# Rotation parts over 29 slots, keys stored once, row stores on ScalarE's queue, maxima ahead of keys, scans and 2-byte tables in the routing

## What is computed

```python
xn = layernorm(x)
Q = (xn @ W_q)              # 16 heads of 16
K = (xn @ W_k)              # 4 heads of 16, each for 4 query heads
V = (xn @ W_v)
scores = rope(Q) @ rope(K).T / sqrt(16)
attn = softmax(scores) @ V @ W_o
top 2 of 8 experts by xn @ W_r, weights = softmax of the two logits
ffn = sum of weight * ((clip(silu(xn @ W_g[e])) * (xn @ W_u[e])) @ W_d[e])
out = x + attn + ffn
```

## Time and profile before

| | us |
|---|---|
| median of 3 runs | 575.77 (574.92 to 575.99) |
| profiled execution | 576.07 |
| its span | 574.3 |
| TensorE busy | 526.5 (92%) |
| VectorE busy | 396.3 (69%) |
| ScalarE busy | 383.5 (67%) |
| GpSimd busy | 173.2 (30%) |
| share of the chain that ended last: TensorE, VectorE, DMA | 73%, 12%, 6% |

### The profile page before, as it was taken

How to read it: one execution, slowest core, us unless ns; L and a number is a source line. 1 busy time by engine, 2 the same in 40 slices (tenths; PEclk the granted TensorE clock), 3 DMA queues, 4 the chain that set the end, 5 groups by cost and what they waited for, 6 DMA issues and landing times.

```text
span 574.3 us, 9921 instructions
## 1 busy us (share of the span) xinstructions
PE 526.5 (92%) x3464; PEld 249.3 (43%) x3464; DVE 396.3 (69%) x920; ACT 383.5 (67%) x548; POOL 173.2 (30%) x208
## 2 busy tenths in 40 slices
PE   1996748897999998999999999999999999999997
PEld 1832324454555554444444444444444444444433
DVE  4578756961666666587788887888888788785123
ACT  3421412431333433799999999999999999998673
POOL 3015854541222210012416422551344342600000
PEclk9997987897999999999999999999999999999999
DMA  8950235566642120310511421422224113100101
GB/s 293 375 184 1 80 133 170 169 183 193 170 138 74 59 62 29 103 38 19 131 47 45 115 58 41 102 65 75 57 58 119 31 57 84 30 2 21 46 29 55
DMA packets 39566, 53.72 MB, mean 94 GB/s; under 512 B 7936, under 2 KB 25728, under 8 KB 39520
## 3 DMA queue, kind: packets, MB, share of 16 engines
q1 hardware_dynamic: 32624, 40.25, 23.9%
q0 software_dynamic: 3408, 9.31, 5.9%
q10 hardware_dynamic: 3488, 3.55, 1.8%
HBM read 36.18 MB, written 16.65 MB: 92 GB/s over the span
## 4 chain that ended last, share of the span: by engine, by line
PE 73%; DVE 12%; DMA 6%; issue 3%; ACT 2%; SPq 2%; POOL 2%; DVEq 0%; ACTq 0%; POOLq 0%
PE bank L1249 21%; PE bank L1239 9%; PE bank L1112 9%; PE bank L1167 8%; PE bank L1129 7%; PE bank L1235 6%; PE bank L1184 4%; PE bank L1285 3%; DMA k_st<-rope_low 3%; PE bank L1122 2%; DMA rows_out<-xn 2%; DVE xn_t L907 2%; DVE xn L983 2%; SPq L378 1%; PE bank L1072 1%
## 5 line engine op out<-in xcount | busy, mean ns | idle before, releaser
L702 ACT ACTIVATE big<-bank 128x1024 f32<-128x1024 f32 x256 | 252.9, 1024 | 18.6 <-PE bank L1239 18.3
L1249 PE MATMUL bank<-big,v_st 128*32 128x256 f32 (+1 forms) x1472 | 148.3, 474 | 2.8 <-DVE xn L983 2.8
L1239 PE MATMUL bank<-qs,kb 64*128 64x512 f32 x512 | 120.0, 408 | 0.7 <-ACT big L702 0.7
L904 DVE TENSOR_REDUCE mx<-bank 128x1 f32<-128x512 f32 x128 | 87.8, 686 | 27.9 <-PE bank L1129 20.1
L899 DVE TENSOR_REDUCE mx<-bank 128x1 f32<-128x512 f32 x128 | 87.9, 687 | 22.1 <-PE bank L1114 20.0
L1167 PE MATMUL bank<-big,xn 128*128 x156 | 82.6, 654 | 15.9 <-ACT xn L671 15.4
L907 DVE CUSTOM_DVE_ANT_0 xn_t<-bank,xn_t 128x512 f32<-128x512 f32 x128 | 87.5, 684 | 4.5 <-PE bank L1129 1.5
L657 ACT ACTIVATE xn_t<-bank 128x512 f32<-128x512 f32 x128 | 76.7, 599 | 20.4 <-PE bank L1114 12.2
L1239 PEld LDWEIGHTS bank<-qs,kb 64*128 64x128 f32 x512 | 57.7, 185 | 19.4 <-ACT big L702 12.3
L1112 PE MATMUL bank<-ka,qs 64*128 64x512 f32 x128 | 63.4, 495 | 0.4 <-DVE mx L904 0.4
L1114 PE MATMUL bank<-ka,qs 64*128 64x512 f32 x128 | 63.3, 495 | 0.0
(11 more groups left out here) (140 smaller groups left out, 611.7 us busy)
## 6 DMA issues: line engine op xcount, KB each, us to landing
qs<-q_hl SPq DMA_DIRECT2D x64, 128.0 KB, 2.7
rows_out<-xn SPq DMA_DIRECT2D x39, 128.0 KB, 2.6
ka<-k_st SPq DMA_DIRECT2D x16, 256.0 KB
kb<-k_st SPq DMA_DIRECT2D x16, 256.0 KB
xs<-in_L_attn_x SPq DMA_DIRECT2D x4, 512.0 KB, 6.3
big<-in_L_ffn_Wg SPq DMA_DIRECT2D x16, 128.0 KB, 6.5
big<-in_L_ffn_Wu SPq DMA_DIRECT2D x16, 128.0 KB, 6.6
big<-in_L_ffn_Wd SPq DMA_DIRECT2D x16, 128.0 KB, 6.5
```

Of the source, the lines that this page charges most:

```text
L702: act.activation(probs[kt % 2][:, 2 * j:2 * j + 2, :].rearrange("p r q -> p (r q)"), st_ps[j][:, :], ACT.Exp, scale=1.0 / math.sqrt(HD)).t ...
L904: nc.vector.reduce_max(mx[h][:, STEPS + k, 1:2], max_bank(v, i), axis=X_AXIS).then_inc(mx_taken, 1)
L1239: last = mm(out[i], kb[p][half[i], kt // QT, keys], qs[q][half[i], j, :], start=False, stop=True, skip_group_check=kt % 2 == 1)
L1249: last = mm(o_ps[32 * r:32 * (r + 1), columns], v_st[p][:, key_block(kt), :], probs[kt % 2][:, r, columns], start=(kt == 0 and columns.sta ...
```

## The change

- A part of the rotation is done in each of slots 1, 3, 5, 7, 9, 11, 14, 17, 20, 23, 26, 29, in four buffers (NB = 4). The order of parts goes by batch. Block 3 is projected partly in slots 0 and 1 and copied by ACT in slot 2.
- A key part is now 128 rows of 512 columns: its lower 64 rows are the keys, the upper ones differences of two kinds. It is stored once (two DMAs for four). Loads read it twice with a broadcast, in 32-row pieces: eight DMAs for `ka` and eight for `kb` instead of two each.
- With the further differences the ones are needed for one key tile in four; three tiles in four use `values_between`, whose cut is at column 128 for 256.
- `store_y` is issued by ACT, for t - 3 in slot t; SP issues the last two.
- SP sends the maxima (`load_m`) ahead of the keys of the next group.
- Routing: totals ahead of ranks, matrices in bf16, two scans for the doubling steps, tables from bf16 operands in pairs, POOL's multiply on DVE, token numbers ahead of the slots' experts.
- PE runs 24 idle products before and 10 after the first transposes; one piece of statistics of the next block is hoisted; the product of values and router has 128 columns for 72.

```diff
+        NB = 4
-        k_st = nc.dram_tensor("k_st", [B, KV, STACK, 2, KCOLS], F32, kind="Internal").ap()
+        k_hl = nc.dram_tensor("k_hl", [B, 2, 2, KV * HD, 2 * HALF], F32, kind="Internal").ap()
...
-        PARTS = [(k, 2) for k in range(BLOCKS - 1)] + [(k, m) for k in range(BLOCKS) for m in range(2)] + [(BLOCKS - 1, 2)]
+        PARTS = [(k, m) for b in range(B) for k, m in ((2 * b, 2), (2 * b + 1, 2), (2 * b, 0), (2 * b, 1), (2 * b + 1, 0), (2 * b + 1, 1))]
-        VECTOR_COS = (3, 5, 7)
+        VECTOR_COS = (3, 5, 7, 9, 11)
+        PART_SLOTS = (1, 3, 5, 7, 9, 11, 14, 17, 20, 23, 26, 29)
+        KEYS_LOAD, FIRST_LOAD, SECOND_LOAD = 13, 14, 18
+        LATE_LOADS = {22: (0,), 25: (1,), 28: (2, 3), 30: (4, 5)}
...
-                    for j, half in enumerate((rope_hi, rope_hi, rope_lo, rope_lo)):
-                        sp.dma_start(k_st[b, :, HD * j:HD * (j + 1), k % 2, :],
-                                     half[n][0:KV * HD, :].bitcast(F32)).then_inc(done, 16)
-            for q in range(NP):
-                store_part(q)
-                if q >= 2:
-                    store_y(q - 2, (q - 2) % 4)
+                    k_rows = [k_hl[b, k % 2, j].rearrange("d (u c) -> u d c", u=2) for j in range(2)]
+                    sp.dma_start(k_rows[0], rope_hi[n][:, :].bitcast(F32)).then_inc(done, 16)
+                    sp.dma_start(k_rows[1], rope_lo[n].bitcast(F32)).then_inc(done, 16)
+            def twice(g, j, half, cols):
+                kv = g % KV
+                return k_hl[g // KV, half, j, HD * kv:HD * (kv + 1), cols].unsqueeze(0).to_broadcast(
+                    [2, HD, cols.stop - cols.start])
...
+                for half in range(2):
+                    for j in range(4):
+                        sp.dma_start(kb[p][2 * HD * j:2 * HD * (j + 1), half, :].bitcast(F32),
+                                     twice(g, j % 2, half, slice(HALF - P, 2 * HALF - P))).then_inc(kb_loaded[p], 16)
...
+            for t in range(SLOTS):
+                q = part_at(t)
+                if q is not None:
+                    store_part(q)
+                if t == KEYS_LOAD:
+                    parts_stored(1)
+                    load_ka(0, 0)
...
                 sp.wait_ge(st_ready, 2 * KT * 2 * g + 1)
-                load_kb(g + 1, 1 - p)
-                if not last:
-                    sp.wait_ge(mx_scored, NI * (2 * g + 2))
-                    load_ka(g + 2, p)
                 for h in range(2):
                     u = 2 * g + h
                     sp.wait_ge(m_turned_ready, u + 2)
                     load_m(1 - h)
+                    if h == 0:
+                        load_kb(g + 1, 1 - p)
+                        if not last:
+                            sp.wait_ge(mx_scored, NI * (2 * g + 2))
+                            load_ka(g + 2, p)
...
+            def store_y(t, i):
+                act.wait_ge(y_copied, t + 1)
+                act.dma_start(rows_out[bass.ts(t, P), :], y_s[i]).then_inc(y_stored[i], 16)
+            for t in range(SLOTS):
+                expert(t, t % 2, first=t == 0, last=t == SLOTS - 1, beside=shared_with(t))
+                if t == 0:
+                    high_part(0)
+                if t == 2:
+                    copy_projected(BLOCKS - 1)
+                if t >= 3:
+                    store_y(t - 3, (t - 3) % 4)
+                if part_at(t) is not None and part_at(t) + AHEAD - 1 < NP:
+                    high_part(part_at(t) + AHEAD - 1)
...
-            link(nc.vector.tensor_copy(sums[0][:, :, :].rearrange(flat), total_ps))
-            src, step = 0, 1
-            while step < 2 * NT:
...
+            link(nc.vector.tensor_tensor_scan(sums_flat, within[:, :, :].rearrange(flat), total_ps, 0.0, ALU.mult, ALU.add))
...
+            link(nc.vector.tensor_tensor_scan(ends[:, :], ones[:, 0:E], n_tiles[:, :], 0.0, ALU.mult, ALU.add))
+            link(nc.vector.tensor_scalar(starts[:, 1:], ends[:, 0:E - 1], float(P), None, ALU.mult))
...
+            nc.vector.tensor_tensor(in_pairs(hot_tile), of_number(place_tile[:, :, :], SW), of_column(slot_row[:, :], 2 * NT),
+                                    ALU.is_equal).then_inc(hot_tile_ready, 1)
+            nc.vector.tensor_tensor(in_pairs(in_tile[:, :, 0, :]), in_pairs(hot_tile), of_number(tile_first[:, :, :], SW),
+                                    ALU.mult).then_inc(in_tile_ready, 1)
...
+            for _ in range(24):
+                mm(idle_ps, ident[:, :], ident[:, :], start=True, stop=True)
...
-            queries_keys(0)
+            queries_keys(0, [0, 1])
...
+            mm(total_ps.rearrange("p (e n) -> p e n", e=E), ones_b[:, :], hot, start=True, stop=True).then_inc(counts_ready, 1)
+            mm(rank_ps.rearrange("p (e n) -> p e n", e=E), earlier[:, :], hot, start=True, stop=True).then_inc(counts_ready, 1)
+            queries_keys(0, [2])
+            queries_keys(1)
+            queries_keys(2, [0])
...
-                if kt % 2 == 0:
+                if kt % QT == 0:
                     for i in parts:
                         mm(out[i], ones_r[half[i], :], ms[v][half[i], j, :], start=True, stop=False)
...
-                values(p, kt, s, u, slice(0, QUART))
+                values(p, kt, s, u, slice(0, P))
...
-                        if kt % 2 == 0 and not last:
+                        if kt % QT < QT - 1 and not last:
```

More of the change, by code:

```diff
@@ L125, in build @@
         n_tiles = sb("n_tiles", [P, E])
-        cum = [sb(f"cum{i}", [P, E]) for i in range(2)]
+        ends = sb("ends", [P, E])
+        starts = sb("starts", [P, E])
+        slot_row = sb("slot_row", [P, SW], BF16)
         slot_no = sb("slot_no", [P, SLOTS, E])
@@ L236, in build @@
         lo_ready = sem("lo_ready")
-        qk_stored = [sem(f"qk_stored{m}") for m in range(3)]
+        qk_stored = [sem(f"qk_stored{m}") for m in range(NB)]
         route = sem("route")
@@ L681, in _ @@
                            ACT.Copy).then_inc(rows_t_ready, 1)
-            for q in range(AHEAD - 1):
-                high_part(q)
-            for t in range(NP):
-                expert(t, t % 2, first=t == 0)
-                if t + AHEAD - 1 < NP:
-                    high_part(t + AHEAD - 1)
-            for t in range(NP, SLOTS):
-                expert(t, t % 2, last=t == SLOTS - 1, beside=shared_with(t))
+            def store_y(t, i):
[11 more added lines that the diff above has]
+                    high_part(part_at(t) + AHEAD - 1)
+            store_y(SLOTS - 3, (SLOTS - 3) % 4)
             act.wait_ge(ht_ready, SLOTS)
@@ L1064, in _ @@
             columns(0)
+            for _ in range(10):
+                mm(idle_ps, ident[:, :], ident[:, :], start=True, stop=True)
             pe.wait_ge(small_loaded, 16 * 6)
+            pe.wait_ge(pool_made, 8)
             for k in range(2 * B):
@@ L1211, in _ @@
             pe.wait_ge(rows_loaded[0], 16)
+            pe.wait_ge(pj_copied, 3 * (2 * B - 1))
             to_columns(0, 0)
-            for t in range(NP):
-                expert(t, t % 4, 16 * ((t + 1) // 4 + 1), first=t == 0)
-            pe.wait_ge(stacks_padded, 5)
-            for t in range(NP, SLOTS):
+            for t in range(SLOTS):
                 if t == SLOTS - SHARED:
-                    pe.wait_ge(ka_loaded[0], 32)
-                expert(t, t % 4, 16 * ((t + 1) // 4 + 1), last=t == SLOTS - 1, beside=shared_with(t))
+                    pe.wait_ge(stacks_padded, 5)
+                    pe.wait_ge(pj_copied, 3 * BLOCKS)
+                    pe.wait_ge(ka_loaded[0], 128)
+                expert(t, t % 4, 16 * ((t + 1) // 4 + 1), first=t == 0, last=t == SLOTS - 1, beside=shared_with(t))
             act_columns(SLOTS - 1, (SLOTS - 1) % 4)
@@ L1238, in scores @@
                         pe.wait_ge(mx_taken, banks)
-                    last = mm(out[i], kb[p][half[i], kt // QT, keys], qs[q][half[i], j, :], start=False, stop=True, skip_group_check=kt % 2 == 1)
+                    last = mm(out[i], kb[p][half[i], kt // QT, keys], qs[q][half[i], j, :], start=False, stop=True, skip_group_check=kt % QT > 0)
                 if parts[-1] == 1:
```

328 lines of the change are left out of this document (165 added, 163 removed).

## The result

The changed kernel takes 556.28 us (median of 4 runs, 555.41 to 557.65); the kernel before took 575.35 beside it. The ratio is 0.967, 95% interval [0.965, 0.970]: 19.1 us faster, where 38.8 were predicted, and above the range of 527 to 550. The profiled execution took 555.41, its span is 553.6, 20.7 less than before.

What follows compares the result with a forecast made beforehand. The prediction took TensorE (PE), the busiest engine, and the holes in its queue as the bound. -14.0 - 23.4 + 5.5 - 5.0 - 1.9 = -38.8 us, from 576.07 and less 0.3, gave 537.0 us; range 527 to 550.

Steps and rivals of the forecast that it cites:

- The stalls on stores go: Slots 0 to 17: without store waits they take 62.1 us instead of 85.5, a term of -23.4 us.
- nobody waits: Attention: key loads in 32-row pieces quadruple SP's issues but have a whole group, 41 us, so they cost nothing.
- The signs named for being wrong: Slots 18 to 29 over 4.6 us each, a DVE down-product copy waiting for a store, or ACT's Silu after an issue.
- Stores stay late: Rival, slots 0 to 17: shared DMA transfer, not issue, delays stores; half the 23.4 us comes, 549 us; chance 0.10.
- Start and routing: Before the slots: earlier clock and shorter routing chain bring first transposes of gathered rows to 44.6 from 58.61, -14.0 us.
- Spreading the parts: Slots 0 to 17: eight rotation parts, every second or third slot, cost 0.5 us each, +4.0 us.
- Slots 18 to 38: Slots beside maxima: four parts and a tail bring DVE to 85 or 95% and cost PE +5.5 us.
- Attention and last group: Attention: fewer products with ones give -5.0 us in the first 14 half-groups and -1.9 in the last group.
- The other cut of the columns: Attention: cutting values at 128 and 384 columns instead of 256 and 256 costs nothing, same columns and count.
- The tiles of 2.68 and 2.47 us: Attention: plain tiles with ones take 2.68 us, split ones 2.47, so eight tiles fall from 20.6 to 20.2 us.
- The rival that ACT's floor would be reached: Rival, attention: ACT runs without holes once pairs are removed, -10 us instead of -5, 532 us; chance 0.14.
- The maxima are sent first ... nothing: Attention group borders: sending maxima ahead of keys gains nothing, since PE has no hole there now.

Runs made afterwards that it cites:

- e4: The changed kernel with key stores as two plain 64-row blocks, first query load in slot 13, and key loads with 16 rows outermost: 534.71 us, ratio 0.928.
- e7: e4 with every row store issued by SP again instead of ACT: 534.57 us.
- f2: The changed kernel with all row stores issued by SP again, key stores left as they are: 572.83 us, ratio 0.992.
- e8: e4 without the 34 idle products: 536.37 us, ratio 0.929.
- e9: e4 with the twelve rotation parts in slots 1 to 12, one in each, instead of spread to slot 29: 561.05 us, ratio 0.973.
- e5: e4 with the split form of values for two key tiles in four instead of three: 535.40 us.
- f1: The changed kernel with the maxima sent behind the keys again, as in the kernel before: 616.89 us, ratio 1.066.
- e3: The changed kernel with key stores as two plain 64-row blocks and the first query load in slot 13: 541.89 us, ratio 0.941.
- e11: The changed kernel with the 16-row key loads alone, key stores and place of the query load unchanged: 561.68 us, ratio 0.973.

## Why the prediction was wrong

**The step that failed** is "The stalls on stores go, because four buffers are reused only eight slots or more later, and because row stores leave SP", in slots 0 to 17, with its twin on the loads, "nobody waits". No term of the sum asks how the new pattern of the key store, two DMAs for four, would be carried. Four such stores in a row on two engines outlast even four buffers (22.93 us, slot 10's hole), and the later one's 6.63 us of issue hold SP before the first query load, whose packets then wait behind it (slot 18's hole). Slots 0 to 17 took 80.1 us for the 62.1 predicted. The predicted 62.1 us came true in e4 (60.1) when nothing but shapes and the place of one load were changed. Shape and place together are worth 21.6 us, more than the whole error of 19.3. The signs named for being wrong did not catch it: no DVE copy waited for a store, and slots 18 to 28 last 4.2 us on the mean. The waits were ACT's and the query load's.

**Stores stay late (549, chance 0.10)** came nearest, with the right place; it had half of the 23.4 us lost there, and 18.0 were, but not by its mechanism. It had row stores late because all transfers share the engines; e4 moves as many bytes, keeps the DMA engines busier, and waits for none. Of its second half, that moved row stores give nothing: true once the key stores are plain (e7), untrue beside the slow ones (f2, 4.4 us in the slots).

**Start and routing** -13.4 for -14.0. DVE's rows for one scan and the tables, which the prediction had at 0.45 and 3.9:

```profile
28.99 0.69 DVE L830 TENSOR_TENSOR_SCAN sums<-within,bank 128x256 f32<-128x256 f32 x1 [0.55 <-PE bank L1133]
34.79 0.82 DVE L864 TENSOR_TENSOR xn<-place_tile,slot_row 128x1280 bf16<-128x1280 bf16 x1
35.65 0.82 DVE L867 TENSOR_TENSOR rope_low<-xn,tile_first 128x1280 bf16<-128x1280 bf16 x1
36.39 2.49 DVE L871 TENSOR_TENSOR xn<-place_row,row_no 128x1024 bf16<-128x1024 bf16 x4
```

The tables sum to 4.13 us. This agrees with the rule that the prediction took from the Trainium skill ("VectorE: DVE Perf Modes", What auto-detection actually checks), two elements a cycle for 2-byte operands with step 1: 1024 elements take 0.62 us (2.49 for four), where the fastest took 1.21 before. The idle products gave more than the 1.2 us taken for the start (2.3 at slot 0, e8).

**Spreading the parts** was right in kind: e9 gives it 15.9 us of slots, and in e4 the 8 parts cost slots 0 to 17 no more than 60.1 - 54.4 - 3.7 = 2.0 us, for the 4.0 predicted.

**Slots 18 to 38** +2.5 for +5.5 (DVE reached 14.91 of 20 us from 160 to 180, 75%, and not the 85 to 95 feared).

**Attention and last group** -4.5 for -6.9. From the first exponential of group 0 to that of group 7 it is 287.1 us for 289.9 before, so the first 14 half-groups gave 2.7 of the 5.0; the rest is the last group, 1.7 for 1.9. The reasons were wrong in two places. The other cut of the columns was costed at nothing, and on e4 it is worth 6.4 us. The tiles of 2.68 and 2.47 us, whose exchange gave 0.42 us per eight tiles, were read from one pair; over the attention of the kernel before, tiles of 2.6 and 2.47 already alternate, and e5 shows that the form does not set the length. Eight tiles take 20.5 us now for 20.7. The rival that ACT's floor would be reached (532) did not hold: about every second tile still takes 2.6, above ACT's 2.46. That ACT keeps PE's gain from counting in full is the better reading, but only the parts' effects are shown, not how each tile of 2.61 us comes about.

**"The maxima are sent first ... nothing"** was the worst misjudgement that did not show in the time. In the kernel before, no wait of PE for maxima shows although the keys go first; within the change it is what the sixteen slow key loads need, and without it the change would have been 6.6% slower than before (f1). It was costed against the old traffic.

## What to carry to other kernels

Read the outermost dimension of both sides of every new DMA before counting DMAs. One of 256 KB that had 2 there kept two engines busy for 6.8 us, everything later on its queue stood behind it, and once several were pending the issuer was held too. So look at what is queued behind it. Cost each part of a change beside the *new* traffic: a reordering that hides nothing today may be what carries the rest of the change. When a stall survives, change the shape, the order and the issuer one by one; here a shape (12.2 us) took the fault away, an order (9.7 us) went round it, and only both together (e3, 14.4 us) showed that they overlapped. Then look for the same shape elsewhere: the key loads had it too (7.2 us).

The best version here is e4 (534.71 us; e7 is the same within 0.2%): the change with plain shapes and the query load one slot earlier, 7.2% faster than the kernel before and 3.9% faster than the change.

## What was unexpected in the hardware

- Stores of 256 KB with 2 rows outermost run on two engines, 6.8 us each, one after the other; the fourth of a row landed 22.93 us after its issue. Behind others of its kind the issue takes up to 6.6 us (0.5 with a single one ahead); as two blocks of 64 rows each, 0.6 us an issue.
- Behind sixteen loads of that shape, 4 KB of maxima took 9.3 us to land. Behind such stores a row store on the same queue took 16.9 us, since the two engines that they share come to it last; on ACT's queue none took over 7.2.
- The attention comes in two kinds, 340 and 350 us, in kernels whose attention has the same instructions. In the long one a tile in most half-groups lasts 2.8 to 3.8 us instead of 2.47, since ACT gets PE's scores up to 1 us late, with no wait of PE on record ahead of them. It stays with a kernel: the runs of each agree within 3 us (f2: within 5). e11 and e4 differ only in key stores and the place of one load, slots earlier. The cause was not found.
